# Expert outputs through DRAM: which pairs go, and which engine issues the reads back

## What is computed

```python
x = x + tanh(g_xattn[0]) * attention(layernorm(x), ctx, ...)
# _layernorm(x) goes into the experts; t = 32 experts, groups of 32 tokens
grouped = x.reshape(B, g, t, d)
logits = jnp.einsum('bgtd,des->bgtes', grouped, controller) + tie
perm = (logits == jnp.max(logits, axis=-3, keepdims=True)).astype(x.dtype)
dispatched = jnp.einsum('bgtd,bgtes->bgesd', grouped, perm)
inner = jax.nn.relu(jnp.einsum('bgesd,desf->bgesf', dispatched, f1) + bias)
intermediate = jnp.einsum('bgesf,esfd->bgesd', inner, f2)
out = jnp.einsum('bgesd,bgtes->bgtd', intermediate, perm)
x = x + tanh(g_ffn[0]) * out
```

## Time and profile before

| | us |
|---|---|
| median of 3 runs | 270.87 |
| lowest and highest | 270.4 and 271.33 |
| the profiled execution, device time | 272.54 |
| its span (first to last instruction) | 270.8 |
| experts in it, from the first L857 to the last L884 | 208.8 to 242.2 |
| combination, from the first L916 on | 243.0 to the end |

### The profile page before, as it was taken

One profiled execution on the slowest core, in us unless ns is written; L12 is line 12 of the kernel. 1 busy time (PEld: TensorE's weight loads), 2 busy tenths in 40 slices (PEclk: granted clock), 3 DMA queues, 4 the chain that ended last, 5 costly groups with the idle time before them and its releaser, 6 DMA issues.

```text
span 270.8 us, 7540 instructions
## 1 busy us (share of the span) xinstructions
PE 224.6 (83%) x2850; PEld 175.8 (65%) x2850; DVE 199.5 (74%) x454; ACT 167.0 (62%) x356; POOL 129.2 (48%) x243
## 2 busy tenths in 40 slices
PE   0465769499788799899989998979998999985994
PEld 0455668387576688687757676857786777773451
DVE  4786738669999969599698887789996555552573
ACT  2642648558657859778577766625887554456562
POOL 5632275555767568857586777654665000000000
PEclk9996868989999999999999999997999999997699
DMA  6735649833253442434310000007996387899724
GB/s 193 228 94 150 176 113 286 248 92 88 75 141 99 119 122 61 121 98 112 82 52 23 7 4 2 4 2 243 394 383 227 85 179 207 233 236 215 174 97 138
DMA packets 32230, 37.91 MB, mean 140 GB/s; under 512 B 4099, under 2 KB 27331, under 8 KB 31939
## 3 DMA queue, kind: packets, MB, share of 16 engines
q1 hardware_dynamic: 31763, 36.85, 47.8%
q10 hardware_dynamic: 432, 0.59, 0.9%
HBM read 18.26 MB, written 6.29 MB: 91 GB/s over the span
## 4 chain that ended last, share of the span: by engine, by line
PE 34%; DVE 19%; POOL 15%; issue 12%; DMA 8%; ACT 6%; SPq 5%; ACTq 0%; POOLq 0%; DVEq 0%
POOL pT L482 6%; PE banks L857 4%; DVE rsum L1268 4%; PE banks L931 4%; PE banks L712 4%; PE banks L732 4%; PE banks L916 3%; PE banks L754 3%; PE banks L875 3%; PE banks L603 3%; DVE nmax L1260 3%; SPq L299 2%; DMA y<-y_rows 2%; DMA w<-in_wattn_dram 2%; POOL xs L476 2%
## 5 line engine op out<-in xcount | busy, mean ns | idle before, releaser
L1260 DVE TENSOR_REDUCE nmax<-banks 128x4 f32<-128x512 f32 x64 | 43.7, 683 | 23.2 <-PE banks L666 22.9
L482 POOL TENSOR_SCALAR_AFFINE_SELECT pT<-pT 128x512 f32<-128x512 f32 x64 | 40.8, 638 | 39.3 <-ACT pT L1023 39.3
L1028 ACT ACTIVATE banks<-cb 128x512 f32<-128x512 bf16 x62 | 37.0, 597 | 12.3 <-DVE nmax L1260 12.2
L1023 ACT ACTIVATE pT<-banks 128x512 f32<-128x512 f32 x64 | 37.5, 586 | 7.5 <-PE banks L683 7.5
L683 PE MATMUL banks<-qst,kst 99*128 99x128 bf16 x256 | 25.8, 224 | 3.9 <-DMA qst<-nT 3.7
L1268 DVE RECIPROCAL rsum<-banks 128x256 f32<-128x256 f32 x16 | 28.0, 1748 | 1.3 <-PE banks L712 1.2
L712 PE MATMUL banks<-pT,va 128*32 128x128 f32 x512 | 27.4, 287 | 0.0
L666 PE MATMUL banks<-kst,qst 96*128 96x128 bf16 x256 | 25.9, 225 | 1.6 <-ACT banks L1028 1.6
L712 PE MATMUL banks<-pT,ones 128*32 128x128 f32 x512 | 25.8, 273 | 0.0
L683 PEld LDWEIGHTS banks<-qst,kst 99*128 99x128 bf16 x256 | 15.5, 100 | 9.1 <-DMA qst<-nT 3.9
L1108 ACT ACTIVATE routed<-banks 128x512 f32<-128x512 f32 x30 | 17.2, 628 | 5.3 <-PE banks L754 5.3
(11 more groups left out here) (133 smaller groups left out, 633.8 us busy)
## 6 DMA issues: line engine op xcount, KB each, us to landing
wx<-in_wexp_dram SPq DMA_DIRECT2D x32, 256.5 KB, 7.3
kst<-kp SPq DMA_DIRECT2D x48, 128.0 KB, 2.4
qst<-qp SPq DMA_DIRECT2D x48, 128.0 KB, 2.4
cT<-in_ctxT_dram SPq DMA_DIRECT2D x8, 256.0 KB, 3.4
y_rows<-ring SPq DMA_DIRECT2D x16, 128.0 KB, 3.3
y<-y_rows SPq DMA_DIRECT2D x4, 512.0 KB, 5.2
wx<-y_rows SPq DMA_DIRECT2D x4, 512.0 KB, 8.3
out_dram<-xs SPq DMA_DIRECT2D x16, 128.0 KB, 2.0
```

The source lines that it names most:

```text
L482: pool.affine_select(p, p, [[0, HC], [1, P]], ALU.is_ge, 0.0, base=0, channel_multiplier=-1)\
L1023: act.activation(pT[:, n % PR, :], BT[n % 2], ACT.Exp, scale=float(D) ** -0.5).then_inc(p_ready, 1)
L1028: act.activation(BS[n % 2], causal, ACT.Copy).then_inc(mask_placed, 1)
L1260: dve.tensor_reduce(nmax[:, b % 2, :].rearrange("p (e j o) -> p e o j", e=2, o=KH)[:, e, o], BS[n % 2].rearrange("p (j t) -> p j t", j=HC) ...
```

## The change

`SENT`, the pairs that go through DRAM, was (0, 1, 3, 4, 6, 7, 9, 10) and is now 0 to 7. `KEPT` and the assignment of experts to pairs follow from it. `load_rows` is moved from SP to GpSimd's program, behind `biases`, and its eight calls stand in the order early 0 to 3, late 0 to 3. SP's program now holds the eight sends and nothing between them. The waits of each read are the same as before.

```diff
-SENT = (0, 1, 3, 4, 6, 7, 9, 10)
+SENT = tuple(range(PAIRS // 2))
...
-            def load_rows(quarter, late):
...
-            send_rows(0)
-            send_rows(1)
-            send_rows(2)
-            load_rows(0, 0)
-            send_rows(3)
-            send_rows(4)
-            load_rows(1, 0)
-            send_rows(5)
-            send_rows(6)
-            load_rows(2, 0)
-            send_rows(7)
-            load_rows(0, 1)
-            load_rows(3, 0)
-            for quarter in range(1, 4):
-                load_rows(quarter, 1)
+            for q in range(len(SENT)):
+                send_rows(q)
...
+            def load_rows(quarter, late):
+
+                for q in (2 * quarter, 2 * quarter + 1):
+                    pool.wait_ge(y_sent[q % YR], 4 * 16 * (q // YR + 1))
+                if late:
+
+                    pool.wait_ge(e_done, PAIRS // 2)
+                pool.dma_start((y0, yw)[late][HALF + quarter::4, :].rearrange("s (k x) -> s k x", k=2),
+                             y_rows[quarter::4].rearrange("s (k l x) j -> s k l (x j)", k=2, l=2)[:, :, late])\
+                    .then_inc(y_loaded[late], 16)
...
             for q in range(BIAS_SETS):
                 biases(q)
+            for late in range(2):
+                for quarter in range(4):
+                    load_rows(quarter, late)
```

## The result

Over 21 executions of each kernel, the median was 271.56 us before and 274.81 us after. The ratio is 1.0075, with a 95% interval from 1.0042 to 1.0107; executions over 1.5% above the fastest of their kernel (12 of the 21 after, for its fastest took 270.4) are left out of the ratio, and the two medians alone would give 1.2%. The forecast of 265.4 and its whole range, to 269.5, were wrong, and so was the sign.

What follows compares the result with a forecast made beforehand. The prediction took PE's work, then the last send and the fourth early read, to bound the kernel. Removing 2.9 us of wait and 2.6 us of slow clock from 270.87 gave 265.4 us, with a range of 264.6 to 269.5.

Steps and rivals of the forecast that it cites:

- The bound: End of the experts to first combination: 2.9 us of PE idle time hang on the fourth early read; without it, start at 245.5.
- The sends come earlier: SP's 32 send issues take 20.5 us without pauses, ending at 233.0 at best, or 234.7 with 1.7 us for stretched issues.
- The reads on GpSimd: Reads issued by idle GpSimd cost about 1 us more; the fourth early read lands at 242.5 to 245.7, removing the 2.9 us wait.
- The rival "slower": Issuing from GpSimd costs several us for each read, slower than before above 3 us; 271 to 276 us, chance 0.12.
- The clock: Without the idle time before the first combination, PE's clock stays at 2.4 GHz, so the slow combinations and turned blocks give 2.6 us.
- What was late next: After the early read: ACT's copies in time, and a stall of 0 to 1.9 us possible for late reads at combine(8), taken as 0.
- The sum: Wait of 2.9 and slow clock of 2.6 us, 5.5 together, taken from the median of 270.87: 265.4 us.
- The waits on buffers: ACT and DVE may wait up to 0.7 us for a send buffer at the eighth pair, hidden from PE.
- The rival of the DMA engines as the limit: DMA engines, not SP's order, set the landing, as reads beside the sends delay them; 269.9 to 270.9 us, chance 0.08.

Runs made afterwards that it cites:

- e8: The kernel after with each of GpSimd's reads cut into four DMAs, runs of 4 KB in place of 16 KB; median 269.10 us, ratio 0.990.
- e4: The kernel after with GpSimd waiting until all eight sends have landed before its first read; one run, 280.6 us.
- e2: The kernel after with the old pairs sent, so only the issuer of the reads (GpSimd) differs from the kernel before; 276.48 us, ratio 1.016.
- e3: First eight pairs sent as in the kernel after, but ScalarE issues the reads between its copies; 277.34 us, ratio 1.019 to the kernel before.
- e12: The kernel after with each read cut into two DMAs of 8 partitions, both runs of 16 KB kept; 273.79 us, ratio 1.006.
- e1: The kernel before with only the pairs changed: first eight sent, SP still issuing the reads; 270.97 us, ratio 0.998.
- e7: First eight pairs sent, sends and reads both issued by GpSimd, in the order of e1; ratio 1.000 to the kernel before.
- e9: The kernel after with each read cut into two DMAs, one for each of a partition's two runs of 16 KB; ratio 0.994.
- e5: e1 with the fourth early read put ahead of the first late read on SP; 270.21 us, ratio 0.998 to the kernel before.
- e6: The kernel before with the fourth early read put ahead of the first late read on SP; 272.24 us, ratio 1.002.
- e10: e8 with the pairs of the kernel before (0, 1, 3, 4, 6, 7, 9, 10); 269.84 us, ratio 0.992 to the kernel before.
- e11: The kernel after with each read cut into two DMAs with runs of 8 KB, on 16 partitions; ratio 0.994.

## Why the prediction was wrong, point by point

**The bound** was read rightly: with the read in time, PE starts its first combination right behind the fifth turned block. e8 shows it, and it shows the 2.49 us of turned blocks and the 1.21 us a batch.

**The sends come earlier**: this step failed. I took 0.64 us an issue, 20.5 for all, and at most 1.7 for stretched ones. It was 30.5. The 1.7 was too small even for before, whose three stretched issues (1.88, 1.33 and 0.99) come to 2.4 over 0.61 each. And the bound came from SP's own order, where a read and the sends behind it are in one queue; there SP went on issuing while the read moved, and what had piled up went out at once behind it. Two windows from about 4 to 6 us behind the issue of the first read, of before and of after, show it (columns as in the earlier trace rows):

```profile
226.00:228.00 2.00, 2.00 (x30) 1.50 (x28) 1.10 (x3) 1.11 (x3) 0.00 (x0) 1.00 1.06 339
```

```profile
225.00:227.00 2.00, 2.00 (x26) 1.45 (x24) 1.17 (x3) 1.11 (x3) 0.00 (x0) 1.00 0.46 135
```

(A packet counts in full where it starts, so a share can pass 1.) In after the DMA engines had a share of 0.46 there: they were not full, the sends had not been issued. Nothing in the trace of before had two queues moving data in this stretch, and I didn't give that a price. Of the 10 us missing, 3.1 come without any read (e4) and 6.9 with the reads of the second queue (e4 against after; e2, e3 and e12 have it, e1, e7, e8 and e9 don't).

**The reads on GpSimd**: the direct cost was right. From the landing of the last send to the read's issue it took 0.5 us, the issue 0.50, the landing 5.12. The 1 us that I took covers it. The rival "slower" put its price on this issue, at 3 us or more, and it was 0.5: right in sign, wrong in its mechanism. What the Trainium skill ("SBUF — State Buffer", section "SBUF: two separate sides") says of DVE holding up GpSimd's descriptors had no part that shows: three of the four early reads were issued in 0.50 us and the first in 0.70.

**The clock**: as a mechanism it was right, and not reached. In after PE waits longer, and the slow stretch costs 1.6 us (0.51, 0.41, 0.44 and 0.27 over the full-clock rows) in place of 2.6. With waits of 0, 1.4 and 2.3 us (e8, e5, e1) the granted clock stayed at 1.00, 2.4 GHz; with 2.6, 2.8 and 2.9 (e7, e6, before) it fell to 0.50.

**What was late next**: I took 0 for the late reads out of 0 to 1.9. In after, e1 and e8 they are no wait. In three kernels whose early read came sooner than before they were: 0.9 us in e5, 1.0 in e10 and 1.1 in e11.

**The sum** failed a second time, apart from the sends. The profile of e8 has all that was forecast: the first combination 36.7 us after the experts' start, as 245.5 - 208.8 had it, no wait at the ninth batch, and the clock at 1.00. It is 6.0 us shorter than that of before, where 5.5 were forecast. Yet the median is 269.10, only 2.5 under before. I took what two stretches of one profiled execution would save as what the median would save; here less than half of it came. Why is open.

**The waits on buffers**: ACT waited 2.3 and DVE 1.9 us at the eighth pair, three times my 0.7. It stayed hidden: PE's experts took 33.4 us, as before.

**The rival of the DMA engines as the limit** was nearest in one point, that the reads beside the sends delay them. The time of 271 to 276 us belongs to the other rival, "slower", which had another cause. The row for 215 to 245, beside that of the earlier trace rows:

```profile
215.00:245.00 30.00, 29.11 (x392) 23.73 (x393) 16.38 (x41) 15.51 (x42) 1.70 (x3) 1.00 0.82 191
```

The share hardly moved (0.82 and 0.84), and the rate fell from 213 to 191 GB/s. That is 0.66 MB less in 30 us, about what before had read by 245: a late read issued at 239.9 and part of the fourth early one, where after had issued neither. So this row tells of the delay and not of its cause; the share of 0.46 above speaks against full engines. The rule of the Trainium skill ("DMA: Bandwidth & Descriptors", section "Issuing engines are not separate DMA queues") that several issuers save the issue time at most gave "no change" here; the measurement was worse than the rule.

**The balance.** The first combination starts 2.2 us later than before, counted from the experts' start, and the slow stretch gives 1.0 back; that is 1.2 us in this pair of profiles, and 1.3 from the experts' start to the end of the span (63.3 against 62.0). The ratio says 2.0 (1.1 to 2.9), and the medians 3.25.

## What to carry to other kernels

When a transfer is moved to another engine's queue to free the first one, look at the issues that stay behind: here a DMA that leaves 32 KB to each engine held up the other queue's issues while it moved. Cutting it turned a loss of 0.75% into a gain of 1.0%. Price stretched issues from a stretch where both queues move data, or say that there is none and widen the range by it. When a wait is about to go, work out the next one with the same care: the late reads cost 0.9 us in e5. And what one profiled execution saves is not what the median saves: 6.0 and 2.5 us in e8.

## What the runs showed of the hardware that I had not expected

- An issue of a send on SP takes 0.61 us, and one of 2.7 to 3.3 comes when a 512 KB read of another queue (GpSimd's or ScalarE's) is in flight (after, e2, e3). In one queue with the read, single issues beside it took at most 0.9 (e1), 1.0 (before) and 1.5 (e5).
- GpSimd issued a send in 0.59 us and a read in 0.50, both no slower than SP (0.61 and 0.53 to 0.58). The packets of its send were of 4 KB, SP's of 1 KB (e7, e4).
- The packets of the sends nearly stop behind a read in one queue too, more than in two (4 and 75 of 1 KB in the same 2 us); with one queue SP goes on issuing.
- Idle time of 2.3 us left TensorE's clock at 2.4 GHz, idle time of 2.6 us in the same place (e7) was followed by 1.2 GHz for 3.4 us.
- What stayed open: why the issue waits, and not the landing alone, why the medians show less than half of what the profile of e8 saves, and why in e4 single issues took up to 2.1 us with no read beside them.
